# First edge stage: edge tiles stationary in the edge network, bias and ReLU moved between engines, the affine part formed transposed

## The reference, cut to what matters

```
msg  = relu(bn(relu(bn(x))[src] @ w1 + b1))          # per edge, 64 columns, a row of mtab
kern = relu(edge_attr_128 @ kw1 + kb1) @ kw2 + kb2   # 32 hidden columns -> (64+1) x 64
kern = kern.reshape(-1, 65, 64)
msg  = einsum('ejk,ek->ej', kern[:, 1:, :], msg) + kern[:, 0, :]
update = segment_sum(msg * edge_weight[:, None], dst, 2000)
```

## Time and profile before

| | |
|---|---|
| runs | 1862.92, 1866.14, 1867.08 us |
| profiled execution, span from its first to its last instruction | 2285.7 us |
| first edge stage in it, from the first gather to the last (54 to 873 us) | 819 us |
[...]
| busy: PE, DVE, ACT, POOL | 1697.3, 951.6, 654.0, 956.8 us |

### The profile page before, as it was taken

How to read it: one execution, slowest core, us unless ns; L and a number is a source line. 1 busy time by engine, 2 the same in 40 slices (tenths; PEclk the granted TensorE clock), 3 DMA queues, 4 the chain that set the end, 5 groups by cost and what they waited for, 6 DMA issues and landing times.

```text
span 2285.7 us, 35842 instructions
## 1 busy us (share of the span) xinstructions
PE 1697.3 (74%) x11519; PEld 981.8 (43%) x11519; DVE 951.6 (42%) x2352; ACT 654.0 (29%) x2149; POOL 956.8 (42%) x1008
## 2 busy tenths in 40 slices
PE   3567677776777765757768787878778887889699
PEld 1344344444444443523434343444334443447448
DVE  5234334433332324724434343444444434446583
ACT  2222222222222221423333233333333323222330
POOL 0656565655555551044444444444444444420000
PEclk8577787787887786867867677777777767679799
DMA  5222222222222221232222222222222222210001
GB/s 181 64 58 58 61 63 57 63 62 63 58 63 62 63 58 38 91 100 65 64 69 63 62 64 69 68 62 69 62 66 70 69 70 69 69 41 19 1 0 36
DMA packets 78941, 142.23 MB, mean 62 GB/s; under 512 B 25483, under 2 KB 33963, under 8 KB 78249
## 3 DMA queue, kind: packets, MB, share of 16 engines
q0 software_dynamic: 40128, 81.99, 14.1%
q1 hardware_dynamic: 38632, 57.99, 8.5%
HBM read 135.22 MB, written 4.67 MB: 61 GB/s over the span
## 4 chain that ended last, share of the span: by engine, by line
PE 43%; another core or an unknown queue 26%; DVE 13%; issue 9%; ACT 6%; DVEq 2%; DMA 1%; SPq 0%; ACTq 0%
PE ps L936 6%; PE ps L944 5%; PE ps L766 4%; PE ps L923 4%; DVE arena L1356 4%; PE ps L954 3%; PE ps L1093 2%; PE ps L1084 2%; PE ps L968 2%; DVE arena L1223 2%; PE ps L1024 2%; PE ps L793 2%; ACT wfT L587 1%; DVE arena L1354 1%
## 5 line engine op out<-in xcount | busy, mean ns | idle before, releaser
L423 POOL DMA_INDIRECT arena<-utab,src x500 | 474.1, 948 | 683.9 <-DVE arena L1356 420.2
L413 POOL DMA_INDIRECT ring<-mtab,src x500 | 480.5, 961 | 391.7 <-issue 185.5
L1223 DVE TENSOR_TENSOR arena<-ps,ring 128x1024 f32<-128x1024 f32 x125 | 153.1, 1225 | 486.8 <-ACT ring L480 232.9
L936 PE MATMUL ps<-arena 64*128 64x256 f32 x1016 | 203.1, 534 | 146.5 <-DVE arena L1356 88.9
L572 ACT ACTIVATE arena<-ps 128x512 f32<-128x512 f32 x193 | 116.7, 604 | 615.8 <-PE ps L923 353.7
L1346 DVE TENSOR_TENSOR arena<-arena,ps 128x40 f32 x512 | 100.4, 196 | 439.2 <-remote 279.7
L954 PEld LDWEIGHTS ps<-small,arena 128*128 128x128 f32 x1270 | 193.6, 234 | 94.6 <-issue 88.0
L766 PE MATMUL ps<-arena,ring 128*64 128x128 f32 x2000 | 197.9, 333 | 41.5 <-issue 41.0
L1356 DVE TENSOR_TENSOR arena<-ps,arena 128x768 f32<-128x768 f32 x252 | 228.4, 948 | 0.0
L923 PE MATMUL ps<-arena 64*64 64x256 f32 (+1 forms) x1544 | 168.3, 513 | 73.5 <-ACT arena L572 54.1
L944 PE MATMUL ps<-arena 128*32 128x512 f32 x1008 | 208.6, 842 | 10.9 <-issue 8.6
(11 more groups left out here) (223 smaller groups left out, 2035.7 us busy)
## 6 DMA issues: line engine op xcount, KB each, us to landing
arena<-in_eaT SPq DMA_DIRECT2D x125, 256.0 KB
ring<-mtab,src POOLq DMA_INDIRECT x500
arena<-utab,src POOLq DMA_INDIRECT x500
arena<-in_rbf SPq DMA_DIRECT2D x132, 32.0 KB
ring<-in_fw SPq DMA_DIRECT2D x2, 1024.0 KB, 5.8
utab<-arena SPq DMA_DIRECT2D x1, 2048.0 KB, 7.5
XT<-in_xT SPq DMA_DIRECT2D x2, 1000.0 KB
arena<-in_x SPq DMA_DIRECT2D x1, 1920.0 KB, 9.6
```

The source lines that it names most:

```text
L413: pool.indirect_dma_start(MR[:, n % 4, k, 0:H], None, mtab, bass.IndirectOffsetOnAxis(ap=src[:, 4 * n + k:4 * n + k + 1], axis=0)).then_in ...
L423: pool.indirect_dma_start(G1[:, n % NSLOT, k, :], None, utab, bass.IndirectOffsetOnAxis(ap=src[:, 4 * n + k:4 * n + k + 1], axis=0)).then_ ...
L936: mm = pe.matmul(ps[:, 2 + h, a * D:(a + 1) * D], R3[hs, c:c + P], m4[hs, :], start=True, stop=True)
L1223: dve.tensor_tensor(RM[:, n % 2, :, :, :], ps[:, 1, 0:P].rearrange("p (t q) -> p t q", t=4).unsqueeze(3).broadcast_to([P, 4, KH, WIN]), SW ...
```

## The change

- `edge_net` is turned round: a tile's edges (128 x 128) are stationary and kw1 (32 columns) is moving. The hidden values come out as edges by 4 x 32 at once, in banks 0 and 1 by turns. `edge_rows` and its transpose go.
- ACT's `relu` goes. DVE's new `pre(n+2)` adds the bias (`kb1t`, 128 x 128) out of PSUM into `PRE` in SBUF. ACT's `edges(n+2)` takes the ReLU from `PRE` into `MR`; it now stands first in ACT's iteration.
- `masks` takes ReLU and product in one, `scalar_tensor_tensor`, four instructions of 256 columns, both tensors in SBUF, in place of one of 1024 columns with one tensor in PSUM.
- `affine` is turned round: `MR` (97 columns) is stationary, `SW` (8 columns, no longer padded) moving. The sums come out transposed, and five groups share 160 columns of bank 4. One copy per bank by ACT (97 x 160) takes the place of two per group; the transposes L750 go, and a memset of `SW` in the prologue.

```diff
             def edge_net(j, n):
                 pe.wait_ge(eal[n % 3], (j * fills(n, QT, 3) + n // 3 + 1) * 16)
-                pe.wait_ge(S["s_relu"], j * QT + n + 1)
+                pe.wait_ge(S["s_pre"], j * QT + max(n - 2, -1) + 2)
                 for t in range(4):
-                    mm = pe.matmul(ps[32 * t:32 * t + 32, 0, 0:P], kw1, EA[:, n % 3, t * P:(t + 1) * P],
+                    mm = pe.matmul(ps[:, n % 2, 32 * t:32 * t + 32], EA[:, n % 3, t * P:(t + 1) * P], kw1,
                                    start=True, stop=True)
-            def edge_rows(j, n):
-                pe.wait_ge(S["s_relu"], j * QT + n + 2)
-                pe.wait_ge(S["s_rc"], j * QT + n + 1)
-                pe.wait_ge(S["s_mask"], j * QT + n + 1)
-                pe.transpose(ps[:, 1, 0:P], RT[:, n % 2, :], ident).then_inc(S["s_tr"], 1)
-            def affine(j, n, part):
...
-                    for t in range(4):
-                        mm = pe.matmul(ps[32 * t:32 * t + 32, 4, 0:CH], SW[:, n // QB % 2, n % QB * 4 + t, :],
-                                       MR[:, n % 4, t, :], start=True, stop=True)
+            def affine(j, n):
+                b, k = divmod(n, QB)
+                pe.wait_ge(S["s_mask"], j * QT + n + 2)
+                pe.wait_ge(S["s_rc"], j * QT + n + 2)
+                pe.wait_ge(gath[n % 4], (j * fills(n, QT, 4) + n // 4 + 1) * 64)
+                if k == 0:
+                    pe.wait_ge(S["s_ae"], j * NB + b + 1)
+                for t in range(4):
+                    c = 32 * k + WIN * t
+                    mm = pe.matmul(ps[0:CH, 4, c:c + WIN], MR[:, n % 4, t, :], SW[:, b % 2, 4 * k + t, :],
+                                   start=True, stop=True)
...
# ScalarE
-                act.activation(RT[:, n % 2, :], ps[:, 0, 0:P], ACT.Relu, bias=kb1c[:, 0:1]).then_inc(S["s_relu"], 1)
-                act.activation(MR[:, n % 4, :, H + 1:], ps[:, 1, 0:P].rearrange("p (t q) -> p t q", t=4),
-                               ACT.Copy).then_inc(S["s_rc"], 1)
+                act.activation(MR[:, n % 4, :, H + 1:], PRE[:, n % 2, :].rearrange("p (t q) -> p t q", t=4),
+                               ACT.Relu).then_inc(S["s_rc"], 1)
+            def affine(j, b):
+                act.wait_ge(S["s_aff"], j * NB + b + 2)
+                act.wait_ge(S["s_con"], j * NB + max(b - 2, -1) + 2)
+                act.activation(AFT[0:CH, b % 2, :], ps[0:CH, 4, 0:160], ACT.Copy).then_inc(S["s_ae"], 1)
...
# VectorE
+                def pre(n):
+                    dve.wait_ge(S["s_e"], j * QT + n + 2)
+                    dve.wait_ge(S["s_rc"], j * QT + max(n - 2, -1) + 2)
+                    dve.wait_ge(S["s_mask"], j * QT + max(n - 2, -1) + 2)
+                    dve.tensor_tensor(PRE[:, n % 2, :], ps[:, n % 2, 0:P], kb1t, ALU.add).then_inc(S["s_pre"], 1)
                 def masks(n):
-                    dve.wait_ge(S["s_rc"], j * QT + n + 2)
+                    dve.wait_ge(S["s_pre"], j * QT + n + 2)
                     dve.wait_ge(S["s_seg"], j * QT + max(n - 2, -1) + 2)
-                    dve.tensor_tensor(RM[:, n % 2, :, :, :],
-                                      ps[:, 1, 0:P].rearrange("p (t q) -> p t q", t=4).unsqueeze(3).broadcast_to([P, 4, KH, WIN]),
-                                      SW[:, b % 2, 4 * k:4 * k + 4, 0:WIN].unsqueeze(2).broadcast_to([P, 4, KH, WIN]),
-                                      ALU.mult).then_inc(S["s_mask"], 1)
+                    for t in range(4):
+                        ins = dve.scalar_tensor_tensor(RM[:, n % 2, t, :, :],
+                                                       PRE[:, n % 2, KH * t:KH * t + KH].unsqueeze(2).broadcast_to([P, KH, WIN]),
+                                                       0.0, SW[:, b % 2, 4 * k + t, :].unsqueeze(1).broadcast_to([P, KH, WIN]),
+                                                       ALU.max, ALU.mult)
+                    ins.then_inc(S["s_mask"], 1)
```

More of the change, by code:

```diff
@@ L189, in build @@
         MR = r0.take(4 * 4 * CH).rearrange("p (g t c) -> p g t c", g=4, t=4)
-        SW = r0.take(2 * 20 * 32).rearrange("p (b t w) -> p b t w", b=2, t=20)
+        SW = r0.take(2 * 20 * WIN).rearrange("p (b t w) -> p b t w", b=2, t=20)
+        kb1t = r0.take(P)
         AFT = r0.take(2 * 160).rearrange("p (b e) -> p b e", b=2)
@@ L275, in build @@
             "s_G", "s_Gm", "s_bv", "s_bvm", "s_h1", "s_h1e", "s_mm", "s_moe", "s_mo",
-            "s_e", "s_relu", "s_tr", "s_rc", "s_mask", "s_seg", "s_oc", "s_aff", "s_ae", "s_con", "s_conc",
+            "s_e", "s_pre", "s_rc", "s_mask", "s_seg", "s_oc", "s_aff", "s_ae", "s_con", "s_conc",
             "s_rmw", "s_step", "s_base",
@@ L333, in _ @@
             ld(w1g.rearrange("p k h -> p (k h)"), A["w1g"], "s_const")
-            for d_, n_ in ((kw1, "kw1"), (kb1c, "kb1c"), (idd, "idd"), (w2g, "w2g"), (wV[0:CH, :], "wV"),
+            for d_, n_ in ((kw1, "kw1"), (kb1t, "kb1t"), (idd, "idd"), (w2g, "w2g"), (wV[0:CH, :], "wV"),
                            (bq, "bq"), (b1c, "b1c"), (b2c, "b2c"), (bfc, "bfc"), (boc, "boc"),
@@ L468, in _ @@
             npass = vload(act)
[L470 to L474 removed]
             def edges(j, n):
[L478 removed]
+                act.wait_ge(S["s_pre"], j * QT + n + 2)
                 act.wait_ge(S["s_seg"], j * QT + max(n - 4, -1) + 2)
[L480 to L495 removed]
+                act.activation(MR[:, n % 4, :, H + 1:], PRE[:, n % 2, :].rearrange("p (t q) -> p t q", t=4),
[4 more added lines that the diff above has]
+                act.activation(AFT[0:CH, b % 2, :], ps[0:CH, 4, 0:160], ACT.Copy).then_inc(S["s_ae"], 1)
             def outer(j, n):
@@ L543, in _ @@
                 for n in range(-3, QT + 7):
+                    if 0 <= n + 2 < QT:
+                        edges(j, n + 2)
                     mix(j, n)
[L545 to L548, removed]
                     if n >= 10 and n % QB == 0:
                         contracted(j, n // QB - 2)
-                    if 0 <= n + 2 < QT:
-                        edges(j, n + 2)
+                    if 0 <= n < QT and n % QB == QB - 1:
+                        affine(j, n // QB)
                     if 0 <= n < QT:
@@ L847, in _ @@
                 for n in range(-3, QT + 6):
-                    if 0 <= n < QT + 2:
-                        affine(j, n, 0)
                     mix(j, n)
@@ L852, in _ @@
                         edge_net(j, n + 3)
-                    if 0 <= n < QT + 2:
-                        affine(j, n, 1)
+                    if 0 <= n < QT:
+                        affine(j, n)
                     b, k = divmod(n - 8, QB)
@@ L1132, in _ @@
             dve.memset(MR[:, :, :, H:H + 1], 1.0)
-            dve.memset(SW, 0.0)
             drv = dr.rearrange("p (q e) -> p q e", q=4)
@@ L1200, in _ @@
             dve.sem_inc(S["s_mask"], 1)
+            dve.sem_inc(S["s_pre"], 1)
             with dve.Fori(0, npass) as j:
@@ L1269, in mix @@
                         dve.tensor_tensor(bvec, ps[:, 6, 0:2], b1c, ALU.add).then_inc(S["s_bvm"], 1)
-                for n in range(-1, QT + 15):
-                    if n + 1 < QT:
+                for n in range(-2, QT + 15):
+                    if n + 2 < QT:
+                        pre(n + 2)
+                    if 0 <= n + 1 < QT:
                         if (n + 1) % QB == 0:
```

24 lines of the change are left out of this document (5 added, 19 removed).

## The result

| | before | changed |
|---|---|---|
| runs of the same chip, median | 1866.19 us (4 runs) | 1880.2 us (4 runs, 1875.15 to 1882.5) |
| ratio, 95% interval | | 1.0083 [1.007, 1.0097] |
| profiled execution, span | 2285.7 us | 1878.1 us |
| first edge stage in it | 819 us | 644.8 us |

The changed kernel is 0.8% slower, 14 us, and 1.0 lies outside the interval. The forecast was slower, 1888 us.

The account below looks back on a forecast made before the run. It took POOL's gathers, at or near their floor of 5.0 us a group, to bound the first edge stage. 1866 us plus 14 for delayed gathers and 8 for PE falling behind gave 1888 us, range 1832 to 1938.

Parts of the forecast that it names:

- the scaled value of 669 us: First edge stage: its profiled 819 us scaled to the unprofiled runs, 44 us above POOL's floor of 625.
- A: First edge stage held at 669 us by the round PE, ACT, DVE, PE; faster by 30, 1836 us; chance 0.30.
- B: POOL's floor holds before and after, gathers fit between DVE's reads; no change, 1866 us; chance 0.16.
- D: Gathers on POOL wait out all four mask instructions, +0.5 us a group, 1928 us; chance 0.08.
- the two terms of the 22 us: First edge stage: gathers delayed on POOL, +14 us, and PE falling behind near half clock, +8 us.
- 0.11 us a group, +14 us: POOL: gathers wait while DVE's new mask instructions read two SBUF inputs; bounds 0 and +90 us.
- +1.0 us a group: PE: mean added work of the new products less the removed lines, +120 us over the first edge stage.
- +8 us for falling behind: PE at half clock needs nearly POOL's 5.0 us a group and the slots don't cover all; bounds 0 and +120.
- The price at full clock: PE: eight new edge records priced at 0.90 us at full clock; at half clock 1.82 us.
- The freed waits at the transposes: PE: idle time ahead of both transposes, 1.46 us a group, goes; the gather is what is late next.
- DVE +50: DVE: masks in four instructions and `pre` add 0.4 us a group, +50 us over the first edge stage, hidden.
- Rival C: First edge stage: PE stays at half clock longer and sets the pace, +75 us, 1941 us; chance 0.12.

Follow-up runs that it names:

- run 2: Changed kernel with `pre` kept in PSUM, so masks read one SBUF input, and the edge network behind `outer` in PE's order; 1875.26 us, ratio 1.0058.
- run 3: Changed kernel with masks as one instruction of 1024 columns, both inputs in SBUF; 1913.53 us, ratio 1.0256.
- run 5: Kernel before with the masks' hidden values read from their SBUF copy instead of PSUM; 1920.09 us, ratio 1.0297.
- run 4: Changed kernel with masks as eight instructions of 128 columns instead of four of 256; 1871.46 us, ratio 1.0046.
- run 12: Kernel before, no edit, profiled once more; 1862.76 us, ratio 1.0008.
- run 10: Changed kernel with masks as eight instructions of 128 columns, and mix and the prologue's sum cut into pieces; 1873.59 us, ratio 1.0033.
- run 7: Changed kernel with three gathers a group instead of four; 1771.86 us, ratio 0.9519 to the kernel before with four.
- run 6: Kernel before with three gathers a group instead of four; 1706.49 us, ratio 0.9155.

## Why the prediction was right

**What bounds the kernel.** That the profile's 420 us were its own, and that POOL is near its floor in the runs, was right; the scaled value of 669 us was an upper end that didn't occur (632 to 634).

**How much the range says.** Little: 1832 to 1938 us holds the centres of A, B and D as well, and slower had a chance of 0.54. What counts is which of the two terms of the 22 us came true. The first did, the second didn't show.

**POOL.** This decided the case. 0.11 us a group, +14 us, was priced from a single stretched gather in the earlier trace rows and a count of hits; 11.1 to 12.5 was measured. That so thin a basis came so close is in part luck, but its parts hold too: 106 hits of 0.135 us were priced (0.85 x 125), and the trace has 94 of 0.12. Runs 2, 3 and 5 show the cause: with one mask input in PSUM the gathers are at 960 ns whatever the rest of the change does; with both in SBUF and one long instruction the kernel before loses 57 us. What was priced is the chance of a hit times half of a read. Both go with the length of a piece, so in this estimate a piece costs the square of its length, and a group's loss falls with the number of pieces: one piece of 1.23 us cost 45 us more than four of 0.36, and eight cost 4.5 less than four (the estimate gives 7; run 4's four long waits are most of the difference). Rival D, waiting out all four, falls by the timeline; B, no delay, by the gathers' mean.

The traces put it on the second SBUF input: a gather of 1.79 us beside a mask with two (run 5), 0.94 beside a mask with one (run 12).

**PE.** +1.0 us a group was priced, 101 us of busy time in 125 groups (0.8) measured. Not all of it is the new products: by their lines L715 and L729 are busy 273 us, the four lines that went (L734, L757, L743, L750) 200, and much of the rest stands in lines that didn't change, as 176 us for L739 where L766 had 160, at a lower clock. The term that followed, +8 us for falling behind, was mis-sized: neither of the two profiles of the changed kernel has a gap. That PE can fall behind is shown by variants, run 2 and run 10, whose gaps lie in the same stretch. From 80 to 120 us the clock was 0.54 (run 2), 0.59 (run 10), 0.64 and 0.63 (changed, twice), and in the kernel before 0.84 and 0.93. The changed kernel got by with 0.64 without a gap. This term is nearly all of the 8 us by which 1888 was too high; the gathers' 14 for at most 12.5 is 1.5 more. Whether unprofiled executions of the changed kernel have gaps can't be seen. The new rows have 0.89/8 = 111 ns a record at full clock, where the row of before had 1.12/10 = 112, and 1.66/8 = 208 ns at half, where it had 2.27/10 = 227. The price at full clock held, the one at half was 9% too high. That the four column positions of L734 worked side by side, and that L715's products do not, is in the records' starts at full clock: L734's come in fours, 7 ns apart, the next four 0.13 us later (`before`, 418.52 and 418.65 us), L715's one by one, 0.11 us apart (changed, 500.65 to 501.32).

The freed waits at the transposes were worth nothing, as reckoned: what comes late now is the gather, and PE simply waits less for it, L757's 128.4 us of before against L729's 40.8 now:

```profile
L757 PE MATMUL ps<-ring 128*32 128x97 f32 x992 | 50.2, 277 | 129.8 <-DMA ring<-mtab,src 128.4 <-DVE arena L1223 1.0
```

```profile
L729 PE MATMUL ps<-ring 128*97 128x8 f32 x992 | 123.9, 251 | 43.0 <-DMA ring<-mtab,src 40.8 <-DVE arena L1200 1.7 <-issue 0.2
```

This is the change's hidden price: 88 us of PE's slack are spent. Run 7 shows it, where the changed kernel is 63 us behind as soon as POOL has less to do.

**DVE and ACT.** DVE +50 priced, +59 measured: `pre` at 0.29 us as priced, and the masks at 1.43 us a group for 1.4. They are hidden:

```profile
L1200 DVE SCALAR_TENSOR_TENSOR arena<-arena,ring 128x256 f32<-128x256 f32 x500 | 179.9, 421 | 202.3 <-PE ps L739 198.4 <-issue 2.3 <-DVE arena L1192 1.2
L1192 DVE TENSOR_TENSOR arena<-ps,ring 128x128 f32<-128x128 f32 x125 | 36.3, 290 | 39.6 <-PE ps L715 36.5 <-issue 0.4
```

The 421 ns is the mean length of an instruction that overlaps the next; four take 1.43 us from start to end. ACT's 73 us less bought nothing.

**Rival C,** a stage run at half clock, had 0.12: the clock fell from 0.86 to 0.79, not under 0.7. What it describes happens for a while in a variant (run 2, 116 to 158 us, at 0.52) and not over half the groups. From 80 to 120 us PE is busy for all 40.0 us at 0.64 in the changed kernel and for 29.7 at 0.93 in the one before; why the clock is lower there, and whether it goes with streaming rather than loading, as the rival's condition has it, no run shows.

## What to carry to other kernels

Where a stage's pace is set by GpSimd's indirect DMAs, look on VectorE for instructions with two SBUF inputs beside them: leave one input in PSUM where it lies there (taking it from SBUF cost 57 us in run 5), or cut the instruction into pieces (here 256 columns instead of 1024 were worth 45 us, 128 another 4.5). Work taken off engines that waited for the gathers was worth nothing here; work added to them is free only until their slack is gone, which a run with fewer gathers shows at once (63 us between runs 6 and 7). And a profile whose span is far above the runs is to be taken again before its waits are believed.

## What the runs showed of the hardware

- A gather that meets a VectorE instruction with two SBUF inputs ends 0.81 us after that instruction's end in runs 5 and 3, 0.82 in the changed kernel and in the earlier trace rows. Undisturbed it takes 0.94 us, so the point at which it waits lies some 0.13 us after its start; that is an estimate from the two figures.
- It gets in between two such instructions of 256 columns that follow each other without a wait, each of the 71 times that it met one with another behind it. I had held it possible that it can't. Among eight of 128 columns, 4 of 83 waited out more than one (run 4).
- Profiled executions of the same kernel before spanned 2285.7, 1851.8 and 1861.2 us; its runs stayed between 1853 and 1868.
